# A gated linear attention, cross attention and feed-forward decoder layer: the prologue of the first two batches reordered, and seven scans placed behind the first maxima

## What is computed

```python
def _L0_attn_ref(inputs, Wq, Wk, Wg1, Wg2, Wv, Wg, bg, Wo):   # H=16, DK=8, DV=16
    q, v = heads(inputs @ Wq), heads(inputs @ Wv)
    k, kg = heads(inputs @ Wk * DK ** -0.5), heads(inputs @ Wg1 @ Wg2)
    gate = jax.nn.silu(inputs @ Wg + bg)
    gt = exp(jax.nn.log_sigmoid(kg) / 16.0)
    # step: state = state * gt[..., None] + k[..., :, None] * v[..., None, :];  out = q . state
    o = _gla_scan(q, k, v, gt)
    o = (o - mean(o)) * lax.rsqrt(var(o) + EPS)               # per head
    return gate * o @ Wo
def _L0_xattn_ref(x, ctx, W_q, W_k, W_v, W_o, b_o):           # 16 heads of 16
    scores = einsum("bqhd,bkhd->bhqk", Q, K) / 4.0
    return einsum("bhqk,bkhd->bqhd", softmax(scores), V) @ W_o + b_o
# feed-forward: sigmoid(xr @ W_r.T) * (relu(xk @ W_k.T) ** 2 @ W_v.T), xr and xk mixed with the token before
x = _layernorm(x + attn(x)); x = _layernorm(x + xattn(x, ctx)); x = _layernorm(x + ffn(x))
```

## Time and profile before

| | |
|---|---|
| median of the runs shown | 532.19 us (3 runs, 528.39 to 536.65) |
| the profiled execution, its own time | 532.64 us |
| its span, first to last instruction | 529.4 us |
| busy: PE, DVE, ACT, POOL | 451.5, 383.4, 292.3, 214.0 us |
| the prologue, until the first score on PE | 93.97 us of the span |

### The profile page before, as it was taken

One profiled execution on the slowest core, in us unless ns is written; L12 is line 12 of the kernel. 1 busy time (PEld: TensorE's weight loads), 2 busy tenths in 40 slices (PEclk: granted clock), 3 DMA queues, 4 the chain that ended last, 5 costly groups with the idle time before them and its releaser, 6 DMA issues.

```text
span 529.4 us, 6244 instructions
## 1 busy us (share of the span) xinstructions
PE 451.5 (85%) x1923; PEld 189.4 (36%) x1923; DVE 383.4 (72%) x642; ACT 292.3 (55%) x516; POOL 214.0 (40%) x213
## 2 busy tenths in 40 slices
PE   8998789889798858899888889888979878897984
PEld 3432434224232113353342323443423423233553
DVE  4988988674778985377997896797548579733285
ACT  3245351543656744645777656546876345688434
POOL 5569793820368970421679772422000011000000
PEclk9999999989989999999999989998989889899998
DMA  7666571521795223124944042220330510000011
GB/s 213 229 176 163 136 192 50 121 61 30 202 216 130 62 70 99 32 70 112 235 111 112 0 102 69 82 60 2 91 81 10 120 51 2 2 0 1 2 40 40
DMA packets 26511, 47.31 MB, mean 89 GB/s; under 512 B 5456, under 2 KB 16368, under 8 KB 26480
## 3 DMA queue, kind: packets, MB, share of 16 engines
q1 hardware_dynamic: 24512, 44.05, 31.7%
q10 hardware_dynamic: 1968, 2.88, 2.2%
HBM read 35.19 MB, written 9.96 MB: 85 GB/s over the span
## 4 chain that ended last, share of the span: by engine, by line
PE 27%; DVE 15%; ACT 10%; issue 4%; DMA 3%; SPq 1%; ACTq 0%; DVEq 0%
PE bank L635 9%; DVE MX L1583 6%; PE bank L696 5%; PE bank L621 4%; ACT PT L1193 4%; PE bank L682 3%; PE bank L673 3%; DMA QS<-mrow 2%; DVE W L1500 1%; DMA x1T<-OT 1%; ACT den L1205 1%; SPq L458 1%; PE bank L912 1%; DVE den L1589 1%; DVE st L1466 1%
## 5 line engine op out<-in xcount | busy, mean ns | idle before, releaser
L1583 DVE TENSOR_REDUCE MX<-bank 128x1 f32<-128x512 f32 x256 | 166.2, 681 | 98.2 <-PE bank L673 94.1
L1193 ACT ACTIVATE PT<-bank 128x512 f32<-128x512 f32 x256 | 146.3, 597 | 113.8 <-PE bank L682 104.0
L682 PE MATMUL bank<-QS,KS 99*128 99x512 bf16 x256 | 97.5, 394 | 17.1 <-ACT PT L1193 12.0
L673 PE MATMUL bank<-KS,QS 96*128 96x512 bf16 x240 | 91.5, 396 | 19.8 <-DVE MX L1583 18.5
L696 PE MATMUL bank<-PT,Vs 128*32 128x512 f32 x512 | 75.1, 661 | 7.7 <-ACT PT L1193 6.0
L1884 POOL TENSOR_TENSOR W<-qT,W 128x512 f32<-128x512 f32 x48 | 62.7, 1309 | 31.5 <-DVE W L1500 20.3
L682 PEld LDWEIGHTS bank<-QS,KS 99*128 99x128 bf16 x256 | 24.1, 99 | 110.8 <-issue 59.4
L1915 POOL TENSOR_TENSOR MP<-MX,zero 128x16 bf16<-128x16 f32 x15 | 3.9, 263 | 110.7 <-DVE MX L1583 77.2
L673 PEld LDWEIGHTS bank<-KS,QS 96*128 96x128 bf16 x240 | 23.8, 100 | 66.2 <-DVE MX L1583 39.9
L1870 POOL TENSOR_TENSOR W<-kT,W 128x512 f32<-128x512 f32 x32 | 43.8, 1372 | 6.7 <-ACT kT L1044 6.7
L1500 DVE TENSOR_TENSOR_SCAN W<-bank,W 128x512 f32<-128x512 f32 x32 | 38.7, 1210 | 0.2 <-ACT bank L1059 0.2
(11 more groups left out here) (218 smaller groups left out, 708.8 us busy)
## 6 DMA issues: line engine op xcount, KB each, us to landing
W<-v_rows SPq DMA_DIRECT2D x20, 512.0 KB, 10.2
k_parts<-parts SPq DMA_DIRECT2D x24, 128.0 KB, 2.4
KS<-k_parts SPq DMA_DIRECT2D x16, 192.0 KB, 3.6
q_parts<-parts SPq DMA_DIRECT2D x24, 128.0 KB, 2.4
QS<-q_parts SPq DMA_DIRECT2D x16, 192.0 KB, 3.6
cT<-in_cT SPq DMA_DIRECT2D x4, 512.0 KB, 3.5
xtok<-in_x SPq DMA_DIRECT2D x4, 512.0 KB, 10.4
W<-v_rows ACTq DMA_DIRECT2D x4, 512.0 KB, 5.9
```

What stands on the lines that cost most here:

```text
L673: pe.matmul(bank(n, b)[:, :], QS[0:NS, h, i * P:(i + 1) * P], KS[0:NS, h, :], start=True, stop=True).then_inc(filled(n, b), 1)
L682: pe.matmul(bank(name, b)[:, :], KS[0:NR, h, kt * P:(kt + 1) * P], QS[0:NR, h, :], start=True, stop=True).then_inc(filled(name, b), 1)
L1193: act.activation(PT[:, n % 2, j, :], bank(name, b)[:, :], ACT.Exp).then_inc(emptied(name, b), 1)
L1583: dve.tensor_reduce(MX[:, NT * h + i:NT * h + i + 1], bank(n, b)[:, :], AX.X, ALU.max).then_inc(emptied(n, b), 1)
```

## The change

On PE value 12 is picked ahead of gate matmul 1 and value 13 ahead of the second sum of batch 0. Six of the eight value matmuls of cross attention stand ahead of the first maximum, in place of 8 `keep_busy`, and two between maxima. The second sum of batch 1 comes behind head 2 instead of head 1; the third and fourth come in the quarters (0, 2) and (1, 0) of the first stage, before their maxima, instead of ahead of the stage and in quarter (0, 3). ACT's copy of the fourth sum and its squares come one quarter later. On ACT the copy of q of batch 1 and all four W loads stand behind the variance's Exp. On DVE the first two scans of batch 1 no longer stand ahead of `scale_half`, 9 instead of 13 scans stand ahead of the maxima; behind the maxima come the gate's log, scans 9 to 11, and scans 12 to 15 one in each quarter of slot 0, behind the quarter's maxima. Two of the four tiles of x1b are made on DVE. On POOL second_product(0) comes behind all multiplies of batch 0, and the memset of the rows of minus one is gone: a DMA on SP brings them from DRAM.

The third sum of batch 1 has moved from ahead of the first score to behind the third, and the fourth from behind the fourth score to behind the fifth. The diff, without the table of banks and the declarations:

```diff
-EARLY_SCANS = 13
+EARLY_SCANS = 9
+LATE_SCANS = 12
@@ SP
+            sp.dma_start(KS[NS:NR, :, :], t["minus"]).then_inc(ks_in, 16)
...
-                sp.wait_ge(ks_set, 3)
+                sp.wait_ge(ks_in, 16)
+                sp.wait_ge(ks_set, 2)
@@ PE, gated_end
-                late = NT * (H + at[0]) + at[1] - (o == 1)
-                if late in SUM_QUARTERS and late >= NT * H:
+                if o == 1 and at in ((0, 2), (1, 0)):
+                    reduce_four(o, 2 + at[0])
+                late = NT * (H + at[0]) + at[1]
+                if o > 1 and late in SUM_QUARTERS:
                     reduce_four(o, SUM_QUARTERS[late])
@@ PE, prologue
                 value_picked(11)
+                value_picked(12)
                 by_feature("gz1", 0, wg, 1, xT)
+                value_picked(13)
                 reduce_four(0, 1)
-                for e in (12, 13, 14, 15):
-                    value_picked(e)
+                value_picked(14)
+                value_picked(15)
...
-                keep_busy("s0.0", 0, 8)
+                for n in range(6):
+                    first_values(n)
                 for h in range(4):
                     for i in range(NT):
                         first_max(h, i)
-                        if h < 2:
-                            first_values(NT * h + i)
+                        if (h, i) in ((0, 1), (0, 3)):
+                            first_values(6 + i // 2)
                         else:
                             keep_busy("s0.0", 0, 1)
-                    if h == 1:
+                    if h == 2:
                         reduce_four(1, 1)
                 keep_busy("s0.0", 0, 6)
                 max_rows(0, 0)
-                keep_busy("s0.0", 0, 8)
-                reduce_four(1, 2)
+                keep_busy("s0.0", 0, 12)
@@ ACT, gated_end
-                if at == (1, 0):
+                if at == ((1, 1) if o == 1 else (1, 0)):
...
-                if at == (1, 1):
+                if at == ((1, 2) if o == 1 else (1, 1)):
@@ ACT, prologue
                 first_decay_ends(1)
-                act.wait_ge(v_out, count(16, 1, 16))
-                act.wait_ge(r_done, count(RQ, 0, 3))
-                for q in (4, 5):
-                    values_in(act, 1, q)
-                first_copy(qT1, "gq", 1)
                 sigmoid_in_bank(0)
...
                 act.activation(var, var, ACT.Exp, scale=-0.5).then_inc(o_rs, 1)
+                first_copy(qT1, "gq", 1)
+                act.wait_ge(v_out, count(16, 1, 16))
                 act.wait_ge(r_done, count(RQ, 0, 4))
-                for q in (6, 7):
+                for q in range(VQ // 2, VQ):
                     values_in(act, 1, q)
...
-                for tt in range(NT):
+                for tt in (2, 3):
                     act.activation(x1b[:, 0, tt, :], xtok[:, tt, :], ACT.Identity, bias=nb[:, tt:tt + 1],
@@ DVE, prologue
                 gate_half(0, o_sq0, 1)
-                first_scan(1, 0)
                 gate_half(1, o_sq, count(1, 0, 1))
-                first_scan(1, 1)
                 dve.wait_ge(o_rs, count(1, 0, 1))
                 scale_half(0)
                 scale_half(1)
...
+                first_scan(1, 0)
                 rest_of("K", K_hi0, 0, 1.0, K_rest0)
-                first_scan(1, 2)
+                first_scan(1, 1)
                 add_half(0)
...
+                for tt in (0, 1):
+                    dve.tensor_scalar(x1b[:, 0, tt, :], xtok[:, tt, :], mv[0][:, tt, 0:1], rs[0][:, tt:tt + 1],
+                                      ALU.subtract, ALU.mult).then_inc(x1_0, 1)
+                first_scan(1, 2)
+                rest_of("K", K_hi0, 1, 1.0, K_rest0)
                 first_scan(1, 3)
-                rest_of("K", K_hi0, 1, 1.0, K_rest0)
+                last_part("K", 1, K_mid0)
                 first_scan(1, 4)
-                first_scan(1, 5)
-                last_part("K", 1, K_mid0)
-                first_scan(1, 6)
                 rest_of("Q", Q_hi0, 0, float(HD) ** -0.5, Q_rest0)
-                first_scan(1, 7)
                 last_part("Q", 0, Q_mid0)
                 rest_of("Q", Q_hi0, 1, float(HD) ** -0.5, Q_rest0)
-                first_scan(1, 8)
+                first_scan(1, 5)
                 last_part("Q", 1, Q_mid0)
-                for e in range(9, EARLY_SCANS):
+                for e in range(6, EARLY_SCANS):
                     first_scan(1, e)
...
                 first_parts()
-                for e in range(EARLY_SCANS, DV):
+                gate_log(1)
+                for e in range(EARLY_SCANS, LATE_SCANS):
                     first_scan(1, e)
-                gate_log(1)
@@ DVE, main loop, behind a quarter's maxima
+                        if s == 0 and LATE_SCANS + NT * n + i < DV:
+                            first_scan(1, LATE_SCANS + NT * n + i)
@@ POOL
-            pool.memset(KS[NS:NR, :, :], -1.0).then_inc(ks_set, 1)
-            pool.wait_ge(ks_set, 1)
...
                 for e in range(DV):
-                    if e == 13:
-                        second_product(0)
                     multiply(0, e)
-                for e in range(1, 5):
+                for e in range(0, 5):
                     second_product(e)
@@ inputs
+        "minus": np.full((NR - NS, H, S), -1, mybir.dt.np(BF16)),
```

More of the change, by code:

```diff
@@ L84 @@
     ("gz0", 1, 5), ("gz1", 1, 2), ("o0", 1, 0),
[1 row of a table added]
     *((f"m{h}.{i}", 0, 3 + i % 2) for h in range(4) for i in range(NT)), ("mr0", 0, 3), ("o1", 1, 0),
-    ("V0", 0, 2), ("V1", 0, 1),
 ]
-EARLY_SCANS = 13
+EARLY_SCANS = 9
+LATE_SCANS = 12
 def dealt(which, slot, tiles_in, heads):
@@ L301, in build @@
         ks_half = first_sem("ks_half"); idb = first_sem("idb"); pick_set = first_sem("pick_set"); wv_set = first_sem("wv_set"); v_half = first_sem("v_half"); ka_in = first_sem("ka_in"); x0_in = first_sem("x0_in"); begun_dve = first_sem("begun_dve"); begun_pool = first_sem("begun_pool")
-        o_sq0 = first_sem("o_sq0"); gate0 = first_sem("gate0"); z_ln0 = first_sem("z_ln0"); z_ls0 = first_sem("z_ls0"); z_sig0 = first_sem("z_sig0"); z_abs0 = first_sem("z_abs0"); z_exp0 = first_sem("z_exp0"); o_gate0 = first_sem("o_gate0"); gated0 = first_sem("gated0")
+        o_sq0 = first_sem("o_sq0"); ks_in = first_sem("ks_in"); z_ln0 = first_sem("z_ln0"); z_ls0 = first_sem("z_ls0"); z_sig0 = first_sem("z_sig0"); z_abs0 = first_sem("z_abs0"); z_exp0 = first_sem("z_exp0"); o_gate0 = first_sem("o_gate0"); gated0 = first_sem("gated0")
         ln0 = first_sem("ln0"); rs0 = first_sem("rs0"); m_step0 = first_sem("m_step0"); m_parts0 = first_sem("m_parts0")
```

## The result

| | before | after |
|---|---|---|
| median | 530.29 us (4 runs, 526.0 to 536.65) | 539.9 us (4 runs, 537.86 to 545.96) |
| the profiled execution, its own time | 532.64 us | 538.18 us |
| its span | 529.4 us | 536.4 us |
| mean granted clock | 0.957 | 0.948 |

The change makes the kernel slower by a ratio of 1.0158, 95% interval 1.0103 to 1.0213, or 8.4 us of 530.29; the two medians are 9.6 us apart. Slower is clear, whether by over 2% is not. The prediction was 540.0 us. An execution's own time is 3.2 us over its span before and 1.8 us after, so I compare single spans only up to marked instructions and leave the totals to the medians.

What follows compares the result with a forecast made beforehand. PE, busy 451.5 of 529.4 us in program order, was taken as the bound. -4.1 up to M, +9.7 behind it and +1.8 for the clock gave +7.4 on 532.64: 540.0 us, range 536 to 544, with rivals 531 to 546.

Steps and rivals of the forecast that it cites:

- M: End of the prologue's sixteenth maximum; predicted at 85.9 instead of 90.00, 4.1 us gained, between 2.0 and 4.6.
- lower clock: PE idle twice for some 4 us behind M: slow clock costs 0.9 at each late sum, 1.8 us in all.
- Step 1: Values 12 and 13 go earlier on PE: DVE's first-batch products and scans end at 42.7 instead of 44.58.
- Step 2: POOL's second_product(0) leaves its multiplies: last first-batch sum starts at 45.7 instead of 46.54, Ln and Exp gain 1.0.
- Steps 3 to 5: From scaling to x1T: scaling at 50.05 (2.65 gained), `nb` at 58.8 (1.7), x1b split, x1T at 62.0 (1.5).
- Step 6: K's last part and SP's DMA queue: QS goes at 70.2, first maximum starts at 74.7, 2.05 us earlier.
- Step 7: Value matmuls replace busywork ahead of the maxima: full clock, holes of first maxima gone, M at 85.9, 4.1 gained.
- Step 8: POOL's memset of KS goes: DVE's cast of 4.77 us shortens, nothing gained; the DMA instead costs SP 0.6.
- After M: POOL's queue delays both late sums; the fourth ends at M + 17.6 instead of M + 7.87, 9.7 us more.
- (a): Faster: prologue's gain kept, fourth sum's delay taken up by PE's later waits, 528.5; this or half of it, chance 0.20.
- (b): Slower by over 2%: lower clock goes on into K's projections and three more sets, 3 us; 545, chance 0.13.
- (c): Maxima start no earlier: four W loads hold up k_parts, only the holes' 1.6 gained; 542.5 us, chance 0.12.

Runs made afterwards that it cites:

- experiment 3: Changed kernel with 19 matmuls without use (fillers) ahead of each of the third and fourth sums: 534.12 us, ratio 1.0026 to the kernel before.
- experiment 4: Changed kernel with POOL's second products 14 and 15 ahead of multiply 9: 537.32 us, ratio 1.0032 to the kernel before.
- experiment 1: Changed kernel with 13 instead of 9 scans ahead of the maxima, as before the change: 532.22 us, ratio 1.001 to the kernel before.
- experiments 5 and 6: Both against the changed kernel: 5, eleven early scans, gate's log later, 529.36 us; 6, products 14 and 15 earlier plus 8 and 17 fillers, 533.43 us.

## Why the prediction was right, and where its steps were off

The end was right, 540.0 against 539.9, in part by luck: the forecast was +7.4 on a base of 532.64, and measured were +8.4 (by the ratio) or +9.6 (by the medians) on a base of 530.29, so the base was 2.35 too high and the change 1.0 to 2.2 too small. The mechanism was right: a gain up to M of about 4, given back more than twice over behind M by the third and fourth sums waiting for POOL, with the lower clock on top. The sum at K0, by after and experiment 3, which differ in the fillers alone:

| | prediction | measured |
|---|---|---|
| M | -4.1 | -3.83 |
| later start of this execution | not foreseen | +0.50 |
| delay behind M at full clock | +9.7 (to the fourth sum) | +8.03 (to K0: 19.81 - 11.78) |
| lower clock | +1.8 | +3.28 (to K0: 23.09 - 19.81) |
| sum | +7.4 | +7.98 |

**Step 1** (scans of batch 0): 43.38, or 42.88 without the lag, against 42.7: right.

**Step 2** was about twice too large: I had the last sum at 45.7, 0.84 earlier, and Ln and Exp gain 1.0. The sum started at 46.68 and Exp ended at 50.90; in experiment 3, whose first projection starts at 7.24 as before, these are 46.17 and 50.39, gains of 0.37 and 0.56. PE itself was the limit: before, the sum had waited for POOL only 0.29 us, as the bracket of its row says, and little more could be gained there. I had taken POOL's lead for PE's.

**Steps 3 to 5**: the scaling came at 50.93 instead of 50.05, since Exp was late (50.43 in experiment 3); `nb` at 59.23 instead of 58.8; the two pieces of x1b took 0.73 together, which is the 0.40 each that I took from the lower end of the earlier trace rows. x1T came at 62.29 instead of 62.0. With the lag of 0.50 taken off, `nb` and x1T are right to 0.2.

**Step 6**: QS at 71.19 instead of 70.2, the first maximum at 75.65 instead of 74.7; half of it is the lag. "SP's queue is rigid" was a little too simple: the six issues of KS took 4.21 us, where the same six took 3.73 before, and SP then stood 0.97 us until q_parts had landed. That DMA and not DVE decides was right (DVE waited 2.17).

**Step 7**: the clock at the first maxima was full as predicted (1.00), the hole 0.83 instead of 1.06. From the first maximum to M it took 11.02 us, predicted 11.2. M came at 86.67 instead of 85.9. In experiment 3, whose first projection started at 7.24 as before, M was 85.91, a gain of 4.09. That this is the predicted 4.1 is luck too: experiment 4 started its first projection at 7.23 and had M at 86.41, with the same order up to there.

**Step 8** (memset): right that nothing was gained. The cast of the earlier trace rows fell from 4.77 us to 0.22 and no time of the path moved. After:

```profile
L1694 DVE CAST identb<-ident x1: 219/219/219, 8.2 to 8.2; 128x128 bf16<-128x128 f32 x1
```

**After M** the queue was counted right, instruction by instruction: POOL starts at M + 3.46 (3.4), the third sum at M + 9.66 (9.6). The fourth was predicted for M + 16.6 and started at M + 17.70 (in experiment 3, at full clock, at M + 16.62). The slow third sum holds up the maximum behind it, and with it scans 14 and 15 on DVE. My sum counted the 0.9 of each slow set and so had 19.4 for where PE goes on; 19.57 was measured.

Two terms were off by nearly the same amount with opposite signs. First, "+5.6 at the same instruction of PE's order" was not the same instruction: the fourth sum had moved back by one quarter, so two maxima and a score that stood behind it now lie ahead of it, and two waits for DVE of 0.51 and 0.21 behind it are gone. From its end to K0 it took 3.91 us before and 2.19 in experiment 3. The delay that counts is 8.0, not 9.7. Second, the lower clock lasted on nearly to K0: behind the fourth sum after needs 3.52 us where experiment 3 needs 2.19, so 1.33 more than the two slow sets and their effect (1.95). The bound of 4.8 held it; the value of 1.8 was too small. So the errors of these two terms, -1.7 and +1.5, cancel.

**The rivals.** (a), the gain kept, falls: the third and fourth sums wait for 7.9 us in all, and no later wait takes the shift up by the product with wo. Behind that, the profiles of before and after differ in further stretches of low clock. After has 0.64, 0.68 and 0.66 in the three pieces of 5 us from 193 to 208, where before, 8 us earlier (185 to 200), has 1.00, 1.00 and 0.67; before has 0.83 from 220 to 230, where after has 1.00 in the like stretch from 227 to 237. In the two profiled executions the shift so goes from 7.99 at wo to 9.0 (the K projection at 212.20 before, at 221.21 after) and back to 7.0 at the end. Whether these stretches belong to the order or to the execution is open, and I did not try it. (b), the clock stays low, was right in kind: it stayed low until shortly before K0 at 109.8 (0.62 from 106 to 110), yet not into the projections, since K0's four matmuls took 1.88 as before. (c), maxima no earlier, falls: the first came 1.08 earlier.

## What to carry to other kernels

Work that is put off behind a landmark must not stand in another engine's in-order queue ahead of something due soon: here two sums waited for POOL 7.9 us in all. Count for each late sum its whole chain (here DVE's log, scans, POOL's products, multiplies), and let products that need nothing new go while the engine is idle. Where PE must wait some 4 us, price the clock too, up to the next instruction that runs at full speed again, and fill the wait with matmuls of no use (here 19 and 19, worth 3.28 us at K0). Compare two orders at an instruction that neither has moved, counted from an early one that both have, and read the bracket of a wait before booking a gain: here it said 0.29, 0.84 was booked and 0.37 came.

## What the runs showed of the hardware

- The granted clock fell after PE had waited 2.42 us for DVE (0.64 from 76.7 to 80.6 us, experiment 1), and with it a maximum's scores took 0.61 us instead of 0.39; the pace of the maxima went from 0.61 to 0.85 us each, though their work on DVE is the same. With the same wait filled, it stayed at 1.00.
- After two waits of 4 us the lower level outlasted the waits: from 106 to 110 us, with PE busy for 4.00 of 4.00 us, the mean was still 0.62. The eight matmuls of P and Vs there took 1.54 us, between the 1.06 and the 1.94 of either level.
- The first projection, the same four matmuls at the same place, took 1.95 or 1.96 us in seven of the nine kernels' profiled executions, at a granted clock of 1.00 from 7 to 11 us, and 3.60 and 3.53 in experiments 5 and 6, at 0.57. By this alone the gate matmul behind it comes 1.65 and 1.70 us later.
- A cast of 128x128 on DVE took 4.77 us while POOL filled rows by memset, and 0.22 us without it.
- POOL's multiply beside the gate's log, 2.25 us before, is gone from this stage: there every multiply after M took 1.26 or 1.27.
